# Cross attention with a feed-forward block in split fp32: one product for queries and keys, another order of slot 3, and another end

## The reference

```python
q = proj(query, Wk, bk); k = proj(key, Wk, bk); v = proj(values, Wv, bv)
scores = einsum('bhqd,bhkd->bhqk', q, k) / sqrt(dk)
allow = tril(ones((S, S), bool), k=mask - 1)
scores_ = softmax(where(allow, scores, NEG)) * allow
distcum = cumsum(scores_, -1); disttotal = sum(scores_, -1)
dist_scores = sqrt(clip((disttotal - distcum) * position_effect, 0))
total_effect = clip(exp(dist_scores * -softplus(gammas)), 1e-5, 1e5)
attn = softmax(where(allow, scores * total_effect, NEG))
query2 = (attn @ v).reshape(B, S, D) @ Wo.T + bo
x = layer_norm(query + query2, ln1_w, ln1_b)
ff = relu(x @ W1.T + b1) @ W2.T + b2
out = layer_norm(x + ff, ln2_w, ln2_b)
```

## Time and profile before

| | |
|---|---|
| median of 3 runs | 1493.36 us (1490.75 to 1493.36) |
| profiled execution | 1497.32 us, span 1495.5 us |
| TensorE busy | 1440.7 us, 96% |
| weight loads | 1205.1 us, 81% |
| VectorE busy | 1080.8 us, 72% |
| ScalarE busy | 1023.1 us, 68% |
| mean granted clock of TensorE | 0.987 |
| mean traffic | 231 GB/s |

### The profile page before, as it was taken

One profiled execution on the slowest core, in us unless ns is written; L12 is line 12 of the kernel. 1 busy time (PEld: TensorE's weight loads), 2 busy tenths in 40 slices (PEclk: granted clock), 3 DMA queues, 4 the chain that ended last, 5 costly groups with the idle time before them and its releaser, 6 DMA issues.

```text
span 1495.5 us, 34270 instructions
## 1 busy us (share of the span) xinstructions
PE 1440.7 (96%) x12896; PEld 1205.1 (81%) x12896; DVE 1080.8 (72%) x3780; ACT 1023.1 (68%) x2626; POOL 156.3 (10%) x180
## 2 busy tenths in 40 slices
PE   5798899999999999999999999999999999999997
PEld 4565788888888888888888888888888888888786
DVE  6997768787787767777776867767686776777533
ACT  4774768777777768677676777767686776866622
POOL 4212010101010010100101010010101001010100
PEclk9898999999999999999999999999999999999999
DMA  8765667666666566665666566566666666665966
GB/s 282 277 245 201 238 224 270 223 254 236 235 249 224 216 208 244 213 239 193 234 221 218 217 217 218 211 222 240 213 225 210 226 217 204 246 215 205 329 242 250
DMA packets 76860, 346.00 MB, mean 231 GB/s; under 512 B 17624, under 2 KB 19416, under 8 KB 44056
## 3 DMA queue, kind: packets, MB, share of 16 engines
q1 hardware_dynamic: 64256, 335.06, 62.9%
q0 software_dynamic: 10208, 7.94, 1.7%
q10 hardware_dynamic: 2232, 0.81, 0.2%
HBM read 316.16 MB, written 27.53 MB: 230 GB/s over the span
## 4 chain that ended last, share of the span: by engine, by line
PE 72%; DVE 11%; ACT 8%; issue 5%; DMA 4%; SPq 0%; POOL 0%; ACTq 0%; DVEq 0%; POOLq 0%
PE bank L226 20%; PE bank L227 19%; PE bank L228 19%; PE bank L492 7%; PE bank L506 5%; DVE w_sb L1351 2%; ACT p_sb L913 2%; ACT xt_hi L974 1%; DVE x_lo L1277 1%; PE bank L526 1%; DVE s_sb L1317 1%; ACT w_sb L902 1%; ACT w_sb L904 1%; DVE w_sb L1341 1%; ACT w_sb L900 1%
## 5 line engine op out<-in xcount | busy, mean ns | idle before, releaser
L226 PE MATMUL bank<-xt_hi,w_ring 128*128 128x256 f32 x1024 | 299.8, 293 | 4.3 <-issue 2.2
L227 PE MATMUL bank<-xt_lo,w_ring 128*128 128x256 f32 x1024 | 291.5, 285 | 0.0
L228 PE MATMUL bank<-xt_hi,w_ring 128*128 128x256 f32 x1024 | 291.3, 284 | 0.0
L1317 DVE CUSTOM_DVE_ANT_0 s_sb<-bank,mask 128x256 f32<-128x256 f32 (+7 forms) x512 | 130.3, 304 | 188.9 <-PE bank L492 188.3
L923 ACT COPY pt_sb<-bank 128x512 f32<-128x512 f32 x192 | 112.0, 583 | 196.3 <-PE bank L506 196.2
L226 PEld LDWEIGHTS bank<-xt_hi,w_ring 128*128 128x128 f32 x1024 | 197.8, 193 | 11.8 <-issue 11.0
L913 ACT ACTIVATE p_sb<-w_sb,nm 128x32 f32<-128x32 f32 (+7 forms) x512 | 205.4, 404 | 2.5 <-DVE nm L1356 2.5
L226 PE MATMUL bank<-w_ring,h_hi 128*128 128x512 f32 x512 | 205.3, 401 | 0.6 <-DMA w_ring<-w_split 0.6
L227 PE MATMUL bank<-w_ring,h_hi 128*128 128x512 f32 x512 | 200.8, 392 | 0.0
L228 PE MATMUL bank<-w_ring,h_lo 128*128 128x512 f32 x512 | 200.7, 392 | 0.0
L227 PEld LDWEIGHTS bank<-xt_lo,w_ring 128*128 128x128 f32 x1024 | 198.2, 194 | 0.3
(11 more groups left out here) (127 smaller groups left out, 2945.2 us busy)
## 6 DMA issues: line engine op xcount, KB each, us to landing
w_ring<-w_split SPq DMA_DIRECT2D x252, 1024.0 KB, 5.1
w_split<-w_ring SPq DMA_DIRECT2D x32, 512.0 KB, 4.9
x_raw<-x_t SPq DMA_DIRECT2D x16, 512.0 KB, 3.6
c_raw<-ctx_t SPq DMA_DIRECT2D x16, 512.0 KB, 4.8
u_sb<-x_rows SPq DMA_DIRECT2D x16, 512.0 KB, 6.0
ring_raw<-w SPq DMA_DIRECT2D x32, 256.0 KB, 5.2
out<-rows SPq DMA_DIRECT2D x15, 512.0 KB, 9.4
zi_row<-zi_out POOLq DMA_DIRECT2D x58, 128.0 KB, 5.1
```

The lines of the kernel that those rows point to most:

```text
L226: nc.tensor.matmul(dst, a_hi, b_hi, start=start, stop=False)
L227: nc.tensor.matmul(dst, a_hi, b_lo, start=False, stop=False)
L228: return nc.tensor.matmul(dst, a_lo, b_hi, start=False, stop=stop)
L1317: m = nc.vector.tensor_tensor_reduce(out=s_sb[:, c % 2, W_AT[b] + 1:W_AT[b] + 1 + WIDTH[b]], in0=s_bank[n % 2][:, at:at + WIDTH[b]], in1=m ...
```

## The change

x and context of a batch, which had tensors of their own, lie side by side in one (`xc_raw`, `xc_hi`, `xc_lo`, each [128, 4, 2, 256]), so that one matmul of 512 columns runs over both. Only the first product of batch 0 stays in two halves. In slot 3 the order of the work on TensorE, ScalarE and VectorE is another. For the last batch, pairs 2 and 5 of the feed-forward weights are not loaded into the ring but into the places of wv and wk, which are free by then; the ring goes on with the pairs that are left. The two last `add_hidden` leave the second half's matmuls of both pairs to the end. In `final`, `totals(last, 3)` stands ahead of `concat(last, 2)`.

```diff
+        SPARE = {2: (wv_hi, wv_lo), 5: (wk_hi, wk_lo)}
+        RING = [(b, p) for b in range(B) for p in range(NP) if b + 1 < B or p not in SPARE]
+        RING_AT = {pair: n for n, pair in enumerate(RING)}
+        def pair_weights(b, p, matrix, r):
+            if (b, p) in RING_AT:
+                at = 4 * matrix + 2 * (RING_AT[b, p] % 2) + r
+                return [w_ring[:, at, part] for part in range(2)]
+            return [SPARE[p][matrix][:, 2 * r + part] for part in range(2)]
...
             def x_in(i):
-                sp.dma_start(x_raw[:], x_t[i]).then_inc(xraw_in, 16)
+                sp.dma_start(xc_raw[:, :, 0], x_t[i]).then_inc(xraw_in, 16)
...
             def w1_behind(b, p):
-                g = NP * b + p
-                if g + 2 < NP * B:
-                    sp.wait_ge(h_mm, g + 1)
-                    w1_pair((p + 2) % NP)
+                at = RING_AT.get((b, p), len(RING))
+                if at + 2 < len(RING):
+                    sp.wait_ge(h_mm, NP * b + p + 1)
+                    w1_pair(at % 2, RING[at + 2][1])
...
+            def spare_pair(p, matrix):
+                home, split = SPARE[p][matrix], (w1_split, w2_split)[matrix]
+                sp.dma_start(home[:].bitcast(F32).rearrange("p (f n) m -> p f (n m)", f=2),
+                             split[p]).then_inc(spare_in[p][matrix], 16)
...
+                        if i == B - 1:
+                            sp.wait_ge(v_mm, made(B))
+                            spare_pair(2, 0)
...
+                        if i == B - 1:
+                            spare_pair(2, 1)
...
+                        if i == B - 1:
+                            sp.wait_ge(qk_mm, NQ * B)
+                            spare_pair(5, 0)
                         if ffn:
                             w2_behind(i - 2, 7)
+                        if i == B:
+                            spare_pair(5, 1)
...
             def queries_keys(i, c):
...
+                else:
                     if c == 0:
-                        pe.wait_ge(xc_lo_ok, 2 * i + n + 1)
+                        pe.wait_ge(xc_lo_ok, 2 * i + 2)
                     for k in range(KT):
-                        mm = three_passes(pj_bank[:, n * S:(n + 1) * S], wk_hi[:, k, cols], wk_lo[:, k, cols],
-                                          hi[:, k], lo[:, k], k == 0, k == KT - 1)
+                        hi, lo = (part[:, k].rearrange("p n s -> p (n s)") for part in (xc_hi, xc_lo))
+                        mm = three_passes(pj_bank[:], wk_hi[:, k, on], wk_lo[:, k, on], hi, lo,
+                                          k == 0, k == KT - 1)
...
-                if g == NP * B - 1:
-                    for t in range(RT):
-                        add(0, t)
-                        add(1, t).then_inc(y_step, 1)
+                if g == NP * B - 2:
+                    add(p, 0, 0)
+                    add(p, 1, 0)
+                elif g == NP * B - 1:
+                    add(p, 0, 0)
+                    add(p, 1, 0).then_inc(y_step, 2)
+                    for q in (p - 1, p):
+                        add(q, 0, 1)
+                        mm = add(q, 1, 1)
+                    mm.then_inc(y_step, 1)
...
                 if now:
                     attend(i, 1)
+                if last:
+                    hidden(i - 1, 1)
                 if ahead:
                     pe.wait_ge(qk_ok, NQ * i + 4)
                     queries_keys(i + 1, 0)
                 if last:
-                    hidden(i - 1, 1)
+                    add_hidden(i - 1, 0)
                 if ahead and i + 1 not in AHEAD:
                     pe.wait_ge(qk_ok, NQ * i + 5)
                     values(i + 1, 0)
-                if last:
-                    add_hidden(i - 1, 0)
...
                 if ahead:
                     x_high(i + 1)
+                    c_high(i + 1)
                 if now:
                     turned(i, 1, 2)
-                if ahead:
-                    c_high(i + 1)
+                if last:
+                    features(i - 1, 0)
+                if now:
                     first_exp(i, 3)
-                if last:
-                    features(i - 1, 0)
...
                     decayed_scores(i, 2)
-                    mask_scores(i, 3, 2)
                 if ahead:
                     inputs_low(i + 1)
+                if now:
+                    mask_scores(i, 3, 2)
...
                 hidden_low(ffn, 3)
+                totals(last, 3)
                 concat(last, 2)
-                totals(last, 3)
```

More of the change, by code:

```diff
@@ L77, in build @@
             wk_raw, wv_raw, wo_raw = (tensor(n, [P, KT, D], F32, loaded) for n in ("wk_raw", "wv_raw", "wo_raw"))
-            x_raw, c_raw = (tensor(n, [P, KT, S], F32, loaded) for n in ("x_raw", "c_raw"))
+            xc_raw = tensor("xc_raw", [P, KT, 2, S], F32, loaded)
             ring_raw = tensor("ring_raw", [P, 8, 2, 512], F32, loaded)
@@ L84, in build @@
         wk_lo, wv_lo, wo_lo = (tensor(n, [P, KT, D], F32R) for n in ("wk_lo", "wv_lo", "wo_lo"))
-        x_lo, c_lo = (tensor(n, [P, KT, S], F32R) for n in ("x_lo", "c_lo"))
+        xc_lo = tensor("xc_lo", [P, KT, 2, S], F32R)
         w_ring = tensor("w_ring", [P, 8, 2, 512], F32R)
@@ L100, in build @@
         wk_hi, wv_hi, wo_hi = (tensor(n, [P, KT, D], F32R) for n in ("wk_hi", "wv_hi", "wo_hi"))
-        x_hi, c_hi = (tensor(n, [P, KT, S], F32R) for n in ("x_hi", "c_hi"))
+        xc_hi = tensor("xc_hi", [P, KT, 2, S], F32R)
         qk_sb = tensor("qk_sb", [P, 2, 2, S])
@@ L214, in build @@
         out_ok = sem("out_ok")
+        spare_in = {p: [sem(f"spare_in{p}_{m}") for m in (1, 2)] for p in (2, 5)}
         out_st = sem("out_st")
@@ L553, in hidden @@
                     pe.wait_ge(h_ok, g)
+                at = RING_AT.get((i, p))
                 if g < 2:
                     pe.wait_ge(ffw_lo_ok, FT - 2 + 2 * p)
+                elif at is None:
+                    pe.wait_ge(spare_in[p][0], 16)
                 else:
-                    pe.wait_ge(w1_in[p % 2], 16 * ((NP // 2) * i + p // 2))
+                    pe.wait_ge(w1_in[at % 2], 16 * (at // 2))
                 for r in range(2):
                     for k in range(KT):
-                        hi, lo = (w_ring[:, 2 * (p % 2) + r, part, P * k:P * k + P] for part in range(2))
+                        hi, lo = (w[:, P * k:P * k + P] for w in pair_weights(i, p, 0, r))
                         mm = three_passes(h_bank[:, S * r:S * r + S], hi, lo, xt_hi[:, k], xt_lo[:, k],
@@ L568, in add_hidden, with add @@
                 pe.wait_ge(h_lo_ok, g + 1)
-                if g >= 2:
-                    pe.wait_ge(w2_in[p % 2], 16 * ((NP // 2) * i + p // 2))
-                def add(r, t):
+                at = RING_AT.get((i, p))
+                if at is None:
+                    pe.wait_ge(spare_in[p][1], 16)
+                elif g >= 2:
+                    pe.wait_ge(w2_in[at % 2], 16 * (at // 2))
+                def add(p, r, t):
                     f = 2 * p + r
@@ L574, in add @@
                         pe.wait_ge(y_ok, RT * (i - 1) + t + 1)
-                    at = slice(P * t, P * t + P)
-                    hi, lo = (w_ring[:, 4 + 2 * (p % 2) + r, part] for part in range(2))
-                    return three_passes(y_bank[t][:], h_hi[:, p % 2, r, at], h_lo[:, p % 2, r, at], hi, lo,
+                    on = slice(P * t, P * t + P)
+                    hi, lo = pair_weights(i, p, 1, r)
+                    return three_passes(y_bank[t][:], h_hi[:, p % 2, r, on], h_lo[:, p % 2, r, on], hi, lo,
                                         f == 0, f == FT - 1)
-                if g == NP * B - 1:
-                    for t in range(RT):
-                        add(0, t)
-                        add(1, t).then_inc(y_step, 1)
+                if g == NP * B - 2:
[8 more added lines that the diff above has]
+                    mm.then_inc(y_step, 1)
                 else:
@@ L587, in add_hidden @@
                         for t in range(RT):
-                            mm = add(r, t)
+                            mm = add(p, r, t)
                     mm.then_inc(y_step, 1)
@@ L978, in x_high @@
                 act.wait_ge(xraw_in, 16 * i + 16)
-                nc.scalar.copy(x_hi[:], x_raw[:]).then_inc(xc_hi_ok, 1)
+                nc.scalar.copy(xc_hi[:, :, 0], xc_raw[:, :, 0]).then_inc(xc_hi_ok, 1)
             def c_high(i):
                 act.wait_ge(craw_in, 16 * i + 16)
-                nc.scalar.copy(c_hi[:], c_raw[:]).then_inc(xc_hi_ok, 1)
+                nc.scalar.copy(xc_hi[:, :, 1], xc_raw[:, :, 1]).then_inc(xc_hi_ok, 1)
             def relu(i, p):
```

38 lines of the change are left out of this document (20 added, 18 removed).

## The result

| | before | changed |
|---|---|---|
| median | 1499.07 us of 20 runs (1490.75 to 1502.78) | 1489.45 us of 20 runs (1485.98 to 1492.57) |
| ratio, 95% interval | | 0.9946, 0.9934 to 0.9959 |
| profiled execution | 1497.32 us, span 1495.5 | 1490.92 us, span 1489.1 |

The change makes the kernel faster, by 8.1 us on the ratio (6.1 to 9.9), against a forecast of 10.9; the median is 7.05 us above the forecast and 0.95 us outside the range. Of these 7.05 us 5.7 are the kernel before: its median was 1493.36 us in three runs and is 1499.07 in twenty. The other 1.3 go by the medians, which are 9.6 us apart; by the ratio 2.8 of the forecast 10.9 were not gained. The interval covers both.

A forecast was written before the change was run, and what follows sets the result against it. TensorE's own list of matmuls bounds the step (busy 88.64 of 88.78 us). Terms 5.0 + 0.1 + 2.5 + 3.7 + 1.0 - 1.1 - 0.3 = 10.9 us, from a median of 1493.36 to 1482.4 us, range 1478.0 to 1488.5.

The forecast's parts named there:

- Product of 512 columns: Queries and keys as 12 matmuls instead of 24: 0.08 us a block, 63 blocks, 5.0 us gained (2.5 to 6.3).
- the middle row: Hidden product's 24 small matmuls (2.87 us) against the values' twelve (2.79): 0.08 us a block, the estimate taken.
- Rival A: Small fixed part of a matmul: 0.03 us a block, 1.9 us there, 7.8 in all, 1485.6; chance 0.12.
- Slot 3: New order at the step's slot 3: one wait of 0.2 us replaces another in 13 steps, 0.1 us gained.
- the failing cover: Hidden p=1 not covering the second input subtraction in slot 3: up to 0.3 us in 13 steps, 4 us.
- rival C: Later c=3 exponentials delay TensorE each step: up to 2.3 us by 13, 30 us lost, 1512; chance 0.07.
- Fill and 1 KB runs: Before the regular steps: batch 1's product waits for both low parts, 1.1 us lost; shorter transfer runs, 0.3 us lost.
- End 1: Totals(last, 3) ahead of concat(last, 2): reciprocal 2.6 us earlier, wait before last output projection goes, 2.5 us gained.
- Rival D: Waits at the end not gained, pair 3's weights late, fill at upper bounds: 6 us gained, 1487.4; chance 0.12.
- End 2: Spare weight pairs in the last batch: pair 2's wait and the 1.2 GHz behind it go, 2.1 + 1.6 = 3.7 us.
- End 3: Last halves apart: last closing chain begins 1.0 us earlier (0.8 to 1.5), despite a new 1.1 us wait before pair 7.
- rival B: New wait before pair 7 brings 1.2 GHz onto the last 18 matmuls: 4.1 us more, 1486.6; chance 0.06.

The follow-up runs named there:

- e1: Changed kernel with the product of queries and keys in halves of 256 columns again; ratio to the kernel before 0.9972.
- e4: Changed kernel with the old order of slot 3 on all three engines, 512 columns kept; ratio to the kernel before 1.0041.
- e5: The changed kernel once more, no edit; ratio to the kernel before 0.9935.
- e16: The kernel before, unchanged, second profile; ratio to the kernel before 1.001, 1249.1 us from the tenth attend to the end.
- e9: e3 with the store of batch 13's rows moved back, behind a load for pair 6 of batch 14; ratio to the kernel before 0.9943.
- e3: Changed kernel with both loads of spare pair 5 issued in the last batch; ratio to the kernel before 0.9943.
- e17: The kernel before, unchanged, third profile; 1253.1 us from the tenth attend to the end, no ratio given.
- e7: The kernel before with only totals(last, 3) put ahead of concat(last, 2); ratio to the kernel before 0.9978.
- e2: Changed kernel without the two spare pairs of weights and their four loads; ratio to the kernel before 0.9969.
- e11: e7 with the store of batch 13's rows moved back as in e9; ratio to the kernel before 0.9969.
- e18: The kernel before, unchanged, fourth profile; 1248.9 us from the tenth attend to the end, no ratio given.
- e6: e3 with the last two additions in the old order, last halves together; ratio to the kernel before 0.9928.
- e10: e9 with the store of batch 13's rows moved forward instead of back; ratio to the kernel before 0.9949.

## Why the prediction was wrong

**The kernel before (not a step of the sum).** "The median of the runs is 1493.36, 4.0 under the profiled one; a saving of this kind is the same in both: 1482.4." This made the largest part of the miss, 5.7 of 7.05 us. Three runs whose middle was near the low end of a kernel that goes from 1490 to 1503 were taken as its level, and the profiled 1497.32 as the exception; it was the other way round. From 1499.07 the same sum would have given 1488.2, 1.3 us under the measured median.

**Product of 512 columns: mis-sized.** Forecast 0.08 us a block, measured 0.055 (e1), between the middle row and the low end of 0.04: from the tenth attend on, 52 blocks gave 2.9 us by that (2.6 with what the new order costs) and not 4.2, and all 63 would give 3.5 and not 5.0. The row may have been the wrong neighbour: 0.08 came from the hidden product beside the values, other operands on either side; why the queries and keys gain less is not shown. Rival A had the right sign and 0.03 as its size. By the rule of the Trainium skill ("TensorE: Matmul & The Clock Gate", section "Wait — 56ns, not 53.3ns?") 1.9 us were to go; the runs stand in the middle between rule and row, 4.6 ns a matmul. (With 1.9 us the sum of 10.9 becomes 7.8; the prediction's 7.9 and 11.0 are a slip of 0.1.)

**Slot 3.** Right as to waits: one of 0.2 us for another. The order cost 0.02 us a step where a gain of 0.01 was put. The price of the failing cover ("up to 0.3 us") looks far too low: e4, which puts back the order on all three engines and not the cover alone, waits 1.28. The exponentials of c=3 begin 2.1 us later in the step (99.80 us after its start against 97.74), their running sum only 0.1 (102.40 against 102.32), and no wait came of it, so rival C was rightly small.

**Fill and 1 KB runs.** The first matmul came 0.41 us later (forecast 0.3), batch 1's product 0.94, which holds the 0.41 and so stands against 1.4. The inputs land in 3.9 us and not 3.6, far from the 6.0 of the rows in 2 KB runs. The sum took off 1.4 us; the first two profiles show none of it, all profiles together 1.7 on average. Whether the end of the kernel sees it is open, as said.

**End 1: the step that failed.** "Ahead of the concat the reciprocal can run at 1402.3, 2.6 us earlier, and the chain behind it keeps its length unless the transfers meet others." The reciprocal did gain 2.65 us, and the transfer did meet another, the store of batch 13's rows. From reciprocal to projection it took 17.07 us and not 14.94, with a load of 10.0 us from issue to landing where before it was 8.4. In the two first profiles 0.5 us came of 2.5; in e5 there was no wait; in half of the four executions of before there was nothing to gain. Rival D had named the slower transfers and priced them at 1.3 us; they took 2.0. Pair 3's weights were not late and the fill was not longer in these two profiles, so that D's 6.0 us in all lies near the measured 6.4 by luck. Of the 4.5 us that the first two profiles stay short of the sum, 2.0 are this term, 1.4 the clock of end 2, and 1.1 the products, the order and the fill together.

**End 2.** Pair 2's wait and the clock behind it went, and pair 3 waits for nothing, as forecast. (The rows gave 7.38 - 5.62 = 1.8 us for the clock and the sum took 1.6; 1.6 is what the stretch cost in the changed kernel, 59.30 us against 57.68 in e5.) But the 1.6 us were counted as the spares' gain, and in the changed kernel they came back at the projection: 2.1 to 2.3 and not 3.7.

**End 3.** 1.0 forecast, 0.96 measured, with the new wait of 1.1 us at 1.08; rival B's slow clock did not come. The reason was half wrong: nearly all of it is pair 7's weights in time.

The terms come to 6.4 us between two executions of the same luck (5.3 between e16 and e5, neither of which waits before the projection), and to 9.8 from before with its waits to e5. The timed runs say 8.1 (6.1 to 9.9). That needs before to have its waits in most executions; all 123 runs of it on record (1490.05 to 1503.00) have a median of 1498.1 us, its profiles without the projection's wait took 1491.5, and of e16's eight runs the profiled one is the fastest, so this is likely, but two of four profiles don't show it.

## What to carry to other kernels

Two things read from one profile may be chance of that execution: a wait that ends with a small transfer, and a stretch at the low clock. Look at what else is issued within a few us of the transfer, and take such a term at half until a second profile has it. If two queues race for the end of a critical chain, move the transfer that nobody waits for behind the other one; here it cost nothing that could be measured (e9 against e3). And take a base from many runs before a saving is put on it.

## What the runs showed of the hardware

- A load of 128 KB on GpSimd's queue, issued 0.27 us or more ahead of a store of 512 KB on SP's, landed after 4.1 to 8.2 us, and TensorE did not wait for its reader, in fourteen profiles of fourteen; issued 0.06 us ahead of it (1404.86 and 1404.92) or up to 1.8 us behind, it landed after 8.4 to 10.0 us and TensorE waited 0.8 to 2.5 us, in six of six. In two of the six (first, e17) it was issued later against the last attend too, so that not the whole wait is the store's.
- A wait's length doesn't tell whether 1.2 GHz follows. Behind 2.51, 2.29 and 2.18 us before the projection nothing came, behind 1.98 us at the same place it did. Behind the wait before pair 2 (1.8 to 2.0 us) it came in the three profiles in which the projection had waited over 2 us 30 us earlier (first, e7, e17), and in none of the four in which it had not (e2, e11, e16, e18). That is a pattern in seven profiles and not an explanation.
- The fill differs from execution to execution. TensorE stood at 1.2 GHz for 20.5 us of it in e6 and 41.0 us in e10, and the tenth attend came at 240.78 and 245.38. In the four profiles of the kernel before it differs by 1.3 us only, and what stands behind it by 4.7.
- The same 24 matmuls of 256 columns took 2.82 us with weights from wv's place (1445.15 to 1447.97) and 2.87 from the ring. In the last batch of the changed kernel the hidden products from the ring take 2.86 to 2.88 us, those of pairs 2 and 5 both 2.82, while the adds take 2.75 us from either place. For one block that is as much as the change got from fewer matmuls; whether the place or the layout of the tile does it is not shown.
